# A sixteen-tile decoder layer on one core: the layer norms' last step on GpSimd, the cross attention's value bias added to the context's values, and a new order on every engine

## What is computed

```python
x = x + min_gru(rmsnorm(x, w_mix), Wg, bg, Wv, bv, Wd, bd)      # gated recurrence along the positions
x = x + sliding_attn(rmsnorm(x, w_attn), Wqkv, Wo)              # 16 heads of 8 features, causal, window 128
x = x + glu_ffn(rmsnorm(x, w_ffn), Wgate, Wup, Wout)            # hidden size 512
y1 = layernorm(x_in + x)
vp = ctx @ Wv.T + bv                                            # the value bias of the cross attention
y2 = layernorm(y1 + softmax(q(y1) @ k(ctx).T / sqrt(128) + mask) @ vp)
out = layernorm(y2 + moe(y2))                                   # 8 linear experts, the best 2 chosen per position
```

## Time and profile before

| what | value |
|---|---|
| time, median of 3 runs | 231.37 us (230.54 to 232.62) |
| the profiled execution's own time | 233.95 us |
| its span, first to last instruction | 232.2 us |
| outside the span | 1.75 us |
| mean granted TensorE clock | 0.975 of full speed |

### The profile page before, as it was taken

The page is one execution under the profiler, slowest core; times in us unless marked ns, Lnnn a source line. Parts: engine busy times, 40 slices in busy tenths (PEclk is TensorE's granted clock), DMA queues, the critical chain, the costliest instruction groups (busy, mean ns, idle before and its releaser), DMA issues. The chain is left out here.

```text
span 232.2 us, 7656 instructions
## 1 busy us (share of the span) xinstructions
PE 212.8 (92%) x2168; PEld 176.3 (76%) x2168; DVE 186.9 (81%) x667; ACT 172.1 (74%) x663; POOL 141.2 (61%) x302
## 2 busy tenths in 40 slices
PE   7789499999999999999999999999999999997940
PEld 3678498889897979887897898888979867975310
DVE  3658277677887978899698999988789977999785
ACT  4899679997788788887588867887867687673450
POOL 5457526666668474677467586764674776564552
PEclk9999979999999999999999999999999999999795
DMA  4986653545244234324024352434141000000000
GB/s 105 255 250 164 147 134 93 145 124 156 57 96 104 54 95 101 106 49 102 5 49 106 73 144 74 108 92 108 47 128 47 28 13 6 11 14 14 11 23 23
DMA packets 33720, 20.09 MB, mean 87 GB/s; under 512 B 20496, under 2 KB 31248, under 8 KB 33680
## 3 DMA queue, kind: packets, MB, share of 16 engines
q1 hardware_dynamic: 32992, 19.35, 32.2%
q10 hardware_dynamic: 688, 0.26, 0.4%
HBM read 14.16 MB, written 5.24 MB: 84 GB/s over the span
## 5 line engine op out<-in xcount | busy, mean ns | idle before, releaser
L2402 DVE TENSOR_REDUCE neg_max<-ps 128x4 f32<-128x512 f32 x64 | 43.0, 676 | 7.1 <-PE ps L902 6.8
L464 POOL TENSOR_TENSOR rs<-ss,neghalf 128x1 f32<-128x1 f32 x48 | 28.4, 595 | 25.6 <-ACT junk L1628 25.3
L1715 ACT ACTIVATE probs<-ps 128x512 f32<-128x512 f32 x64 | 38.5, 605 | 4.7 <-PE ps L922 4.5
L464 POOL TENSOR_TENSOR lrs<-mv,neghalf 128x1 f32<-128x1 f32 x48 | 26.3, 552 | 21.8 <-DVE mv L2493 8.7
L1052 PE MATMUL ps<-w_moe,y2T 128*128 128x512 f32 x64 | 34.0, 621 | 0.0
L969 PE MATMUL ps<-xT,guT 128*128 128x128 f32 x256 | 33.2, 276 | 0.0
L969 PEld LDWEIGHTS ps<-xT,guT 128*128 128x128 f32 x256 | 30.9, 192 | 1.3 <-ACT xT L1744 1.0
L525 POOL TENSOR_SCALAR_AFFINE_SELECT probs<-probs 128x600 f32<-128x600 f32 x32 | 24.4, 761 | 8.8 <-ACT probs L1715 8.5
L900 PE MATMUL ps<-k_stack,q_stack 125*128 125x128 bf16 x256 | 25.3, 222 | 2.8 <-DMA k_stack<-qk_scratch 2.8
L922 PE MATMUL ps<-q_stack,k_stack 128*128 128x128 bf16 x256 | 24.8, 219 | 0.0
L900 PEld LDWEIGHTS ps<-k_stack,q_stack 125*128 125x128 bf16 x256 | 18.5, 100 | 5.5 <-issue 4.0
(11 more groups left out here) (156 smaller groups left out, 588.1 us busy)
## 6 DMA issues: line engine op xcount, KB each, us to landing
q_stack<-qk_scratch SPq DMA_DIRECT2D x48, 96.0 KB
k_stack<-qk_scratch SPq DMA_DIRECT2D x48, 96.0 KB
qk_scratch<-qk_parts SPq DMA_DIRECT2D x16, 192.0 KB, 2.2
ctx_sb<-in_ctx_dram SPq DMA_DIRECT2D x4, 256.0 KB, 4.3
qk_scratch<-qk_parts SPq DMA_DIRECT2D x16, 64.0 KB, 2.0
out_dram<-x_all SPq DMA_DIRECT2D x16, 64.0 KB, 1.5
x_all<-in_x_dram SPq DMA_DIRECT2D x2, 256.0 KB, 3.1
raw<-in_L_ffn_Wi_dram SPq DMA_DIRECT2D x1, 512.0 KB, 6.3
```

The lines of the kernel that those rows point to most:

```text
L464: nc.gpsimd.tensor_tensor(dst, src, neghalf[:], ALU.pow).then_inc(S[rsd], 1)
L1715: nc.scalar.activation(probs[:, b, n, :, :], view("probs", 4 * k + n), ACT.Exp, scale=HD ** -0.5).then_inc(S["att_p"], 1)
L2402: nc.vector.tensor_reduce(neg_max[:, b, QUARTER * n:QUARTER * n + QUARTER], view("scores", 4 * k + n), AX_X, ALU.max, negate=True).then_in ...
```

## The change

Four things are done at once.

1. The last step of the three layer norms goes from VectorE to GpSimd, directly behind `power` in most places. The operation is the same `tensor_scalar` with two per-partition columns. 48 instructions change engine.
2. `xat_residual` goes, and `ctx_bias(k)` adds the bias to tile k's context values after `ctx_copy_kv(k)`: again 16 `tensor_tensor` of 128x128 on GpSimd. `xat_values` waits for it, `xat_out` reads `y1`.
3. Waits that other waits imply are left out: some 25 calls in VectorE's helpers, 23 in ScalarE's, nine in GpSimd's, two in TensorE's; most were waits for tile k-2's reader.
4. Every list of calls and the table of banks are new. `load_out` and `load_small` come later, `load_ctx` earlier, six dummy products are placed after the first nine instead of one.

```diff
-            def power(src, dst, ready, k, rsd, used):
-                after_all(pool, (ready, k + 1), (used, k - 1))
+            def power(src, dst, ready, k, rsd):
+                after(pool, ready, k + 1)
                 nc.gpsimd.tensor_tensor(dst, src, neghalf[:], ALU.pow).then_inc(S[rsd], 1)
...
+            def layernorm_apply(n, k, b, src, dst, rsd, done):
+                after(pool, rsd, k + 1)
+                nc.gpsimd.tensor_scalar(dst, src, mv[:, n, b, 0:1], lrs[:, n, b:b + 1], ALU.subtract, ALU.mult).then_inc(S[done], 1)
...
+            def xat_layernorm(k):
+                b = k % 2
+                after(pool, "moe_high", k - 1)
+                layernorm_apply(1, k, b, z[:, 1, b, :], y2[:, b, :], "xat_rs", "xat_y2")
...
-            def xat_residual(k):
-                b = k % 2
+            def ctx_bias(k):
                 if k == 0:
                     pool.wait_ge(S["w_small"], 48)
-                after(pool, "ffn_y1", k + 1)
-                after(pool, "xat_z", k - 1)
-                nc.gpsimd.tensor_tensor(y1b[:, b, :], y1[:, b, :], xbv_sb[:], ALU.add).then_inc(S["xat_y1b"], 1)
+                nc.gpsimd.tensor_tensor(ctx_kv[:, k, 1, :], ctx_kv[:, k, 1, :], xbv_sb[:], ALU.add).then_inc(S["ctx_vb"], 1)
...
             def xat_values(k):
                 after(pe, "xat_pT", k + 1)
+                after(pe, "ctx_vb", k + 1)
...
-            def layernorm_apply(n, k, b, src, dst, rsd, done):
-                after(dve, rsd, k + 1)
-                nc.vector.tensor_scalar(dst, src, mv[:, n, b, 0:1], lrs[:, n, b:b + 1], ALU.subtract, ALU.mult).then_inc(S[done], 1)
```

More of the change, by code:

```diff
@@ L49 @@
-    "w_out": "1",
[L50 to L60, removed]
@@ new lines, in _ @@
+            ffn_power(2)
+            ctx_bias(2)
+            xat_ln_power(1)
+            xat_layernorm(1)
+            max_split(5)
+            ctx_bias(3)
+            keep_causal(4, 0)
+            keep_causal(4, 1)
+            ctx_bias(4)
+            moe_add(0)
+            ctx_bias(5)
+            qkv_power(10)
+            ctx_bias(6)
+            ffn_power(3)
+            ctx_bias(7)
+            moe_add(1)
+            keep_causal(5, 0)
+            ffn_residual(3)
+            ffn_ln_power(2)
@@ new lines, in _ @@
+            qk_low(8)
+            xat_ln_power(3)
+            xat_layernorm(3)
+            keep_causal(6, 1)
+            moe_add(2)
+            ffn_residual(5)
+            keep_causal(7, 0)
+            moe_ln_power(1)
+            qkv_power(11)
+            keep_causal(7, 1)
+            moe_add(3)
+            xat_ln_power(4)
+            xat_layernorm(4)
+            qk_low(9)
+            ctx_bias(8)
+            moe_layernorm(1)
+            ffn_ln_power(5)
+            ffn_layernorm(5)
@@ L1291, in _ @@
-            att_turn(5)
+            att_values(2)
+            scores_turned(3, 0)
+            xat_turn_probs(0)
+            ffn_down(1)
+            scores_turned(3, 1)
+            max_turn(4)
+            att_back(2)
+            gru_gates(11)
+            xat_values(0)
+            scores(5, 0)
+            att_turn(2)
+            gru_gates(12)
+            xat_turn(1)
+            att_project(2)
+            scores(5, 1)
+            xat_scores(1)
+            scores_turned(3, 2)
+            scores(5, 2)
@@ new lines, in _ @@
+            moe_turn(0)
+            scores_turned(3, 3)
+            scores(5, 3)
+            moe_logits(0)
+            scores_turned(4, 0)
+            xat_turn_probs(1)
+            moe_experts(0, 0)
+            xat_values(1)
+            scores_turned(4, 1)
+            att_values(3)
+            scores_turned(4, 2)
+            ctx_turn(12)
+            moe_experts(0, 1)
+            moe_turn(1)
+            ffn_turn(2)
+            scores_turned(4, 3)
+            att_back(3)
+            moe_experts(1, 1)
@@ L1359, in _ @@
+            ffn_up(7)
+            ffn_down(6)
+            scores_turned(8, 2)
+            scores(9, 2)
+            ffn_down(7)
+            gru_turn_back(14)
+            scores_turned(8, 3)
+            scores(9, 3)
+            moe_experts(5, 1)
+            v_project(10)
+            xat_turn(6)
+            scores(10, 0)
             att_values(8)
```

2705 lines of the change are left out of this document (1293 added, 1412 removed).

## The result

| | before | after |
|---|---|---|
| time, median of 4 runs each | 231.8 us (230.54 to 232.62) | 235.94 us (235.8 to 236.12) |
| ratio after to before | | 1.0177, 95% interval 1.013 to 1.0223 |
| the profiled execution | 233.95 us, span 232.2 | 236.12 us, span 234.4 |

What follows compares the result with a forecast made beforehand. Bound: TensorE's own work in the middle, a start losing 14 us, an end of one chain. Terms -2.5 - 3.0 + 0.5 - 2.5 = -7.5 took 233.95 to 226.45; less 2.58, median 223.9 us, range 218 to 228.

Steps and rivals of the forecast that it cites:

- I take 400, since two columns have to be fetched: Layer norm step on GpSimd: priced at 400 ns, 48 x 0.40 = 19 us more, GpSimd 160 us or 69%.
- The ends of the term: Bounds on one layer norm step's length on GpSimd: 0.31 us and, for the unknown fetch, 0.9 us.
- the case of a long step: A layer norm taking 0.9 us on GpSimd, making GpSimd the bound: 235.4 us, chance 0.11.
- signs of being wrong: GpSimd's step above 0.8 us, TensorE waiting for y often in the middle, or a stack later than 30.
- Rival 2: GpSimd becomes the bound: layer norm 0.9 us, GpSimd 184 us, total 235.4; decides from about 0.8 us; chance 0.11.
- Rival 3: GpSimd takes twice VectorE's time for a layer norm step, 0.69 us: 225.8 us, chance 0.13.
- That one was 2.58 above the median ..., so I forecast 223.9: Passing from 226.45 for an execution like the profiled one to a median, against the earlier median of 231.37.
- The start's term: Before the first scores: the 2.79 us stack wait is filled and the clock need not fall, -3.0 us (-5 to +2).
- Middle: Middle tiles: a freer VectorE returns a third of TensorE's 8.2 us lag, -2.5 us (-7 to +2).
- End: Tile 15's chain: `ffn_down(15)` to `moe_turn(15)` from 11.95 to 9.6 us, -2.5 us (-4.5 to +1.5).
- Bias: Bias on the context's values: 16 GpSimd additions go and 16 of the same shape come, 0.
- Waits: Some 350 fewer wait instructions on VectorE, 7 us of its queue beside TensorE's work: 0 (-3 to 0).

## Why the prediction was wrong

The new order with four lengths of the step, nothing else changed; only the last row computes the whole layer:

| step on GpSimd | operations | time | ratio to before (95%) |
|---|---|---|---|
| 0.30 us | multiply, add, constants | 227.32 | 0.9813 (0.9747 to 0.988) |
| 0.45 | add, multiply, columns | 227.99 | 0.9856 (0.9807 to 0.9904) |
| 0.65 | subtract, multiply, constants | 231.89 | 1.0006 (0.9968 to 1.0044) |
| 0.80 | subtract, multiply, columns (after) | 235.94 | 1.0177 (1.013 to 1.0223) |

**The step that failed** is "I take 400, since two columns have to be fetched". The row it leaned on, `gru_a` at 307, was of the right engine and shape but of another pair of operations, and I took the fetch for the only difference. Measured: 150 ns for the columns, 350 for the subtraction. At 0.45, near the length that I assumed, the kernel takes 227.99; at the real one 235.94. That is 8.0 us of the miss of 12.0. The ends of the term, 0.31 and 0.9, did hold the truth, but the case of a long step had a chance of only 0.11. Two of the prediction's signs of being wrong came: an instruction above 0.8 us, and TensorE waiting for y.

**Rival 2 is what happened.** "GpSimd becomes the bound" gave 235.4; measured 235.94. Its place was right: GpSimd 179.0 us (rival: 184), 9.4 of 10 in a stretch of the middle, turns of y waiting. That its number came so near is partly luck: it was made for a step of 0.9 us, and it priced the middle at 6 without a row, where the lag grew by 4.3 (8.5 to 12.8). Its point of decision was wrong: the break-even with before lies near 0.65 us, not 0.8, and the price is no straight line: 0.7 us of total from 0.30 to 0.45, 3.9 from 0.45 to 0.65, 4.05 from 0.65 to 0.80 (by the ratios 0.4, 1.5 and 1.7%). Rival 3 had the length at 0.69 and 225.8 for it; 0.65 gives 231.89. Its rule (the Trainium skill, GPSIMD Engine Reference, section "Elementwise — side-by-side cycle accounting", GpSimd about half as fast) is stated for two tensor inputs, and the step has one; still it came nearest: 802 to VectorE's 346 is 2.3. But add, multiply at 452 is only 1.3 of that same 346 (VectorE's add, multiply was not measured), so that one factor for the engine does not give the length; the operations do.

**The base.** "That one was 2.58 above the median ..., so I forecast 223.9" takes the same time away twice. The start's term (-3.0) was read from an execution in which TensorE stood 2.79 us for the stack and ran at 0.86 behind it. In three other profiles of the old order that wait is 1.60 (steps on GpSimd), 1.37 (the bias alone) and 2.66 (short step). In all three the clock stays at 1.00 from 30 to 40, even behind the 2.66 (TensorE's timeline of that run at `scores(0, 0)` and `scores(4, 0)`, then its stretch):

```profile
28.00 0.38 PE L968 MATMUL ps<-k_stack,q_stack 125*128 125x128 bf16 x4 [2.66 <-DMA k_stack<-qk_scratch]
...
55.64 0.39 PE L968 MATMUL ps<-k_stack,q_stack 125*128 125x128 bf16 x4
```

```profile
30.00:40.00 10.00, 9.48 (x95) 8.32 (x95) 7.87 (x20) 9.93 (x42) 6.08 (x17) 1.00 0.57 141
```

So the fall to 0.86 does not come with every wait of that length. `scores(4, 0)` starts at 54.65, 54.33 and 55.64 in these three, at 57.41 in the profiled execution; by that its lag is 11.1 to 12.4 us, not 14.1. So much of what the new start seemed to save is just what made the profiled execution long. The new order's profiled execution has no such wait and no such excess (with add, multiply: 227.9, median 227.99). Counted so, the base is 2.6 us of the miss. That the wait varies from execution to execution is shown by the four profiles; that wait and clock made up the whole excess of 2.58 is argued from them, since only one execution of a kernel is profiled. The record of 71 other executions of before agrees in size: the 30 with a mean granted clock of 0.987 or more have a median of 230.9 us, the 11 below 0.979 one of 232.9.

**The other terms**, in the kernel with 0.45 us (add, multiply), where the step is near what I assumed, against the profiled execution of before:

- Start: forecast -3.0 and +0.5 for dummy products. Lag at `scores(4, 0)` 14.1 to 10.4, less the 1.1 us by which the list of products has grown: -2.6. Right, against that execution; against the lags of 11.1 to 12.4 it is between +0.4 and -0.9, next to nothing.
- Middle: forecast -2.5. `scores(4, 0)` to `att_values(15)` loses 8.5 before, 17.8 - 10.4 = 7.4 now: -1.1, less than half of it. With 0.30 us it is 6.2, so -2.3.
- End: forecast -2.5. From `ffn_down(15)` to the end of the span 14.5 us of lag before, 11.7 now: -2.8. Right, and for the stated reason: 9.5 us from `ffn_down(15)` to `moe_turn(15)`, where 9.6 was forecast:

```profile
205.70 1.06 PE L1050 MATMUL ps<-outT,hidden 128*128 128x128 f32 x8
...
215.17 0.27 PE L904 MATMUL ps<-ident,y 128*128 128x128 f32 x1
```

- Bias: 0, measured nothing that can be told. Waits: 0, measured 0.8 us, not told from nothing.

Against the profile of the bias alone in the old order (230.88 us) the same reckoning gives +0.4 for the start, -1.7 for the middle and -2.0 for the end.

In sum, the span falls by 6.0 us (232.2 to 226.2) where -7.5 was forecast. So of the miss of 12.0 us, 8.0 is the step's length, 2.6 the base, and 1.5 the rest, above all the middle.

**Where the time of after went**, kernel with 0.45 us against after: `scores(4, 0)` 10.4 and 10.1, `att_values(15)` 17.8 and 22.9, `ffn_down(15)` 19.0 and 25.4, the span 30.7 and 38.9. Some 5 us are lost in the middle and 3 behind it. GpSimd had 48 x 0.35 = 17 us more to do, so that half of it shows.

## What to carry to other kernels

A step that moves to another engine is priced by a row with the same engine, shape and operations; where no row has all three, forecast both ends, and give the far one its weight. An operation's price may hang on the pair: it is worth trying add for subtract, if a sign can be had for less than it saves (here the negation cost 2.7 to 3.8 us of the 8.0). A time saved that was read from one long execution is not to be saved again when passing to the median. And an engine's busy share says little of how near it is to being the bound when short steps of the critical chain stand in its queue: GpSimd went from 71% of the span (step 0.45 us) to 74% (0.65), and the gain was gone.

## What the runs showed of the hardware

GpSimd's `tensor_scalar` on 128x128 f32 takes 301 ns (multiply, add, constants), 451 (the same, columns), 466 (two products, columns), 609 and 635 (a product or a subtraction alone, one column), 649 (subtract, multiply, constants) and 802 (subtract, multiply or multiply, subtract, columns). With a product beside it, a subtraction takes 0.35 us more than an addition, with columns and with constants alike; two columns take 0.15 us more than two constants; a product alone takes longer than two products. The same subtract, multiply with two columns has a median of 346 on VectorE, which hinted at none of it.
